# A mixer and a recurrence put into one program, and four small products moved from VectorE to ScalarE

## The reference

```python
x = norm(x + mamba2(x, W_in, conv_w, conv_b, A_log, D_skip, dt_bias, norm_w, W_out))
x = norm(x + bounded_linear(x, weight, scale))     # out = x @ weight * scale, its row norm squashed by tanh and held under 0.99
x = norm(x + rg_lru(x, w_y, w_x, conv, w_ig, w_ag, a_param, w_out))
x = norm(x + gated_ffn(x, gate_w, up_w, down_w))   # integer weights minus 128, silu(g) * u
```

## Time and profile before

| | us |
|---|---|
| median of 3 runs | 1288.69 (1288.57 to 1290.66) |
| the profiled execution | 1291.74 |
| its span, from the first instruction to the last | 1290.0 |
| busy: TensorE, its weight loads, VectorE, ScalarE, GpSimd | 1109.6, 970.0, 779.7, 523.8, 312.8 |
| mean granted clock of TensorE | 0.933 of 2.4 GHz |

### The profile page before, as it was taken

How to read it: one execution, slowest core, us unless ns; L and a number is a source line. 1 busy time by engine, 2 the same in 40 slices (tenths; PEclk the granted TensorE clock), 3 DMA queues, 4 the chain that set the end, 5 groups by cost and what they waited for, 6 DMA issues and landing times. The chain is left out here.

```text
span 1290.0 us, 18165 instructions
## 1 busy us (share of the span) xinstructions
PE 1109.6 (86%) x6912; PEld 970.0 (75%) x6912; DVE 779.7 (60%) x1335; ACT 523.8 (41%) x934; POOL 312.8 (24%) x450
## 2 busy tenths in 40 slices
PE   5689889898989885477899999992899999999998
PEld 5568777877878774367898888982687887878876
DVE  4598888888888888345777766754343323223213
ACT  4564536354545543145545655452231231230320
POOL 1011112020202115144433334410131231230330
PEclk9789999999989996778999999997799999999999
DMA  4403031212213042510000111000900201101001
GB/s 173 161 17 120 10 128 41 88 50 80 88 42 109 4 160 83 211 67 1 33 4 31 33 34 34 14 20 20 347 1 25 73 1 33 65 0 41 25 1 49
DMA packets 41585, 81.15 MB, mean 63 GB/s; under 512 B 7456, under 2 KB 13472, under 8 KB 39456
## 3 DMA queue, kind: packets, MB, share of 16 engines
q1 hardware_dynamic: 41504, 80.06, 17.9%
HBM read 67.19 MB, written 12.85 MB: 62 GB/s over the span
## 5 line engine op out<-in xcount | busy, mean ns | idle before, releaser
L1715 DVE SCALAR_TENSOR_TENSOR d_h<-d_psu,d_us,d_sg 128x512 f32<-128x512 f32 x64 | 48.1, 751 | 168.7 <-PE d_psu L1756 160.0
L1677 ACT ACTIVATE d_sg<-d_psg,d_gs 128x512 f32<-128x512 f32 x64 | 44.1, 690 | 245.3 <-PE d_psg L1756 245.3
L1652 POOL TENSOR_TENSOR d_hl<-d_h,d_hh 128x512 fp32r<-128x512 f32 x64 | 82.8, 1293 | 167.7 <-ACT d_hh L1666 167.7
L552 DVE SCALAR_TENSOR_TENSOR a_xs<-a_xpre,a_cvec,a_xs 128x256 f32<-128x256 f32 x192 | 100.8, 539 | 9.2 <-ACT a_xs L446 4.6
L1768 PE MATMUL d_pso<-d_wd,d_hh 128*128 128x512 f32 x256 | 101.0, 395 | 2.9 <-POOL d_hl L1652 2.9
L1768 PE MATMUL d_pso<-d_wd,d_hl 128*128 128x512 f32 x256 | 100.5, 392 | 0.0
L326 POOL TENSOR_TENSOR a_sg<-a_sg 128x512 f32<-128x512 f32 x16 | 21.2, 1327 | 251.2 <-ACT a_sg L438 251.2
L649 DVE TENSOR_TENSOR_SCAN a_L<-a_L,a_ident 128x512 f32<-128x512 f32 x64 | 81.7, 1338 | 0.5
L789 PE MATMUL a_psr<-a_xth,a_wgh 128*128 128x256 f32 x256 | 74.7, 292 | 7.6 <-DVE a_wgl L543 7.6
L789 PE MATMUL a_psr<-a_xth,a_wxh 128*128 128x256 f32 x256 | 74.9, 293 | 7.0 <-DVE a_wxl L543 7.0
L789 PE MATMUL a_psr<-a_xth,a_wgl 128*128 128x256 f32 x256 | 72.6, 284 | 0.0
(11 more groups left out here) (302 smaller groups left out, 3237.4 us busy)
## 6 DMA issues: line engine op xcount, KB each, us to landing
a_L<-decays SPq DMA_DIRECT2D x16, 1024.0 KB, 4.8
a_xf<-in_x SPq DMA_DIRECT2D x16, 256.0 KB, 2.8
a_xr<-in_x SPq DMA_DIRECT2D x16, 256.0 KB, 2.7
tokens<-a_xr SPq DMA_DIRECT2D x16, 256.0 KB, 2.0
c_xb<-tokens SPq DMA_DIRECT2D x16, 256.0 KB, 2.8
tokens<-c_xb SPq DMA_DIRECT2D x16, 256.0 KB, 2.0
d_xin<-tokens SPq DMA_DIRECT2D x16, 256.0 KB, 4.5
d_wd_codes<-in_down_w SPq DMA_DIRECT2D x4, 1024.0 KB, 15.7
```

The source lines that it names most:

```text
L552: ins = dve.scalar_tensor_tensor(out=dst, in0=src[:, k:k + T], scalar=vec[:, k:k + 1], in1=dst, op0=ALU.mult, op1=ALU.add)
L1652: pool.tensor_tensor(hl[:, m, :], h32[:, m % 2, :], hh[:, m, :].bitcast(F32), ALU.subtract).then_inc(s_hl, 1)
L1677: act.activation(sg[:, m % 2, :], ps_g[:, m % 2, :], ACT.Silu, scale=gs[:, m:m + 1]).then_inc(s_sg, 1)
L1715: dve.scalar_tensor_tensor(out=h32[:, m % 2, :], in0=ps_u[:, m % 2, :], scalar=us[:, m:m + 1], in1=sg[:, m % 2, :], op0=ALU.mult, op1=ALU. ...
```

## The change

It does five things.

1. **One program.** `mamba2` and `bounded_rg_lru` no longer open blocks of their own; each returns a function per engine, and `build` runs them behind each other in one block. No barrier, no reset of semaphores lies between them. They share PSUM (one tensor of 8 banks, cut the same way as far as the steps go), the identity and the constants. The places in SBUF are laid out anew so that the first tiles of the recurrence lie on tiles of the mixer that are free early.
2. **The last step takes in the front of step 0**, from `turn_in` to `turn`, and the softplus: the calls are written between those of the mixer on each engine. All six weights go through the ring of pieces; the last two are split at the end of the front, on ScalarE and then GpSimd.
3. **`tokens` is moved from VectorE to ScalarE**: 8 operations of 128x64 with a scale from `dt` take the place of one of 128x512.
4. **Weights at the start.** The loads of w_bc and of three pieces of w_x go ahead of the small vectors, the halves of w_x ahead of the first `bc`, the halves of w_gate between the first evictions and taps.
5. **Waits.** A helper `Order` lets an engine wait for the instruction that it has just issued. It replaces single semaphores; in `scan` and `cumulate` there is now such a wait behind each scan instead of one behind the last.

The core of the diff (changed indentation left out):

```diff
+class Order:
+    def __call__(self, ins):
+        self.count += 1
+        ins.then_inc(self.sem, 1)
+        self.eng.wait_ge(self.sem, self.count)
...
 # mamba2, SyncE
-            load_piece(0)
+        for i in range(4):
+            load_piece(i)
             for dst, src in ((cvec, conv), (nega, ...), (dtb, ...), (dsk, d_skip), (nrm, norm_w)):
                 sp.dma_start(dst, src).then_inc(s_small, 16)
-            for i in range(1, NG):
+        for i in range(4, NG):
                 load_piece(i)
...
             sp.wait_ge(s_gate, 4 * NS)
-            for i, (raw, src, _, _) in enumerate(following):
-                sp.dma_start(raw, src).then_inc(s_next[i], 16)
+        following_stage["load_x"](0)
+        following_stage["constants"]()
+        load_piece(NW)
+        load_piece(NW + 1)
+        following_stage["load_x"](1)
+        load_piece(NW + 2)
+        load_piece(NW + 3)
+        sp.wait_ge(s_yp, R * C * NS)
+        sp.wait_ge(s_su, G * C * NS)
+        load_piece(NW + 4)
+        load_piece(NW + 5)
             store(NS - 1)
...
 # mamba2, ScalarE
+        def tokens(s, q):
+            act.wait_ge(s_xtr, 4 * s + q + 1)
+            ...
+            for j in range(C):
+                for i in range(HQ):
+                    h = q * HQ + i
+                    ins = act.activation(xdt[:, j, h * HD:(h + 1) * HD], ps_t[:, q % 2, 2 * j + i // 2, i % 2 * HD:(i % 2 + 1) * HD],
+                                         ACT.Copy, scale=dt[:, j, h:h + 1])
+            ins.then_inc(s_xdt, 1)
...
+            else:
+                high_piece(NW)
+                high_piece(NW + 1)
+                following_stage["turn_in"](0)
...
+        square(C * NS - 2)
+        high_y(C * NS - 1)
+        square(C * NS - 1)
+        following_stage["softplus"](0)
+        following_stage["square"](0)
+        high_piece(NW + 2)
+        following_stage["tanh"](0)
+        high_piece(NW + 3)
+        following_stage["softplus"](1)
+        following_stage["turn"](0)
+        following_stage["turn_in"](1)
+        high_piece(NW + 4)
+        high_piece(NW + 5)
...
 # mamba2, VectorE
                 for q in range(Q):
-                    dve.tensor_tensor_scan(own, own, ident4..., 0.0, ALU.mult, ALU.add).then_inc(s_sc, 1)
+                order(dve.tensor_tensor_scan(own, own, ident4..., 0.0, ALU.mult, ALU.add))
...
-            def tokens(s, q):
-                dve.wait_ge(s_xtr, 4 * s + q + 1)
-                dve.tensor_tensor(xdt[:, :, 256 * q:256 * q + 256]..., ps_t[:, q % 2]..., dt[:, :, heads(q)]..., ALU.mult).then_inc(s_xdt, 1)
...
 # mamba2, GpSimd
+        low_piece(NW)
+        low_piece(NW + 1)
+        following_stage["constants"]()
+        tree(C * NS - 2)
+        tree(C * NS - 1)
+        scale(C * NS - 2)
+        scale(C * NS - 1)
+        following_stage["bound"](0)
+        norm(C * NS - 2)
+        following_stage["bounded_norm"](0)
+        norm(C * NS - 1)
+        low_piece(NW + 4)
+        low_piece(NW + 5)
...
 # mamba2, TensorE
-            pe.wait_ge(s_const, 15 + HQ)
+        pe.wait_ge(s_const, 2)
             turn(0)
+        pe.wait_ge(s_const, 15 + HQ)
...
+            else:
+                following_stage["turn_in"](0)
...
+        following_stage["project"](0)
+        out_proj(C * NS - 2, 0)
+        ...
+        out_proj(C * NS - 1, 1)
+        following_stage["turn"](0)
+        following_stage["turn_in"](1)
...
 # bounded_rg_lru, what begins behind the mixer
+        def main():                     # SyncE
+            sp.wait_ge(*last["output"])
+            sp.dma_start(bo, b_out.partition_broadcast(P)).then_inc(s_bias, 16)
+            load_x(2)
```

More of the change, by code:

```diff
@@ L973, in bounded_rg_lru @@
-def bounded_rg_lru(nc, signals, x_in, x_out, scale, vectors, b_out, fill, W, late, space, ahead):
+                        last = pe.matmul(ps_y[:, r, 2 * g + i, :], S[rows(r), b, g, i * P:(i + 1) * P], ex[rows(r), g, cols(j)],
+                                         start=(g, i) == (0, 0), stop=False, skip_group_check=True)
+            last.then_inc(s_in, 1)
+            for r in range(R):
+                pe.wait_ge(s_mx, R * n + r + 1)
+                for g in range(G):
+                    for i in range(HQ):
+                        h = g * HG + r * HQ + i
+                        last = pe.matmul(ps_y[rows(i % 2), r, 2 * g + i // 2, :], xdt[:, j, h * HD:(h + 1) * HD], L[j][:, h, :],
+                                         start=False, stop=True, skip_group_check=True)
+                last.then_inc(s_yp, 1)
@@ new lines, in tensor @@
+        pe.wait_ge(s_const, 2)
+        turn(0)
+        pe.wait_ge(s_const, 15 + HQ)
+        pe.wait_ge(s_wlo, 1)
+        bc(0)
+        turn_z(0)
+        x_proj(0, 0)
+        x_proj(0, 1)
+        for s in range(NS):
+            x_proj(s, 2)
+            if s:
+                out_proj(C * s - 2, 0)
+            turn_a(s)
+            if s:
+                out_proj(C * s - 2, 1)
+            x_proj(s, 3)
+            gram(s)
+            if s:
+                sum_sq(C * s - 2)
+                sum_sq(C * s - 1)
+            x_turn(s, 0)
+            if s:
+                out_proj(C * s - 1, 0)
+                out_proj(C * s - 1, 1)
+            x_turn(s, 1)
+            gate(s, 0)
+            x_turn(s, 2)
+            gate(s, 1)
+            x_turn(s, 3)
+            gate(s, 2)
+            gate(s, 3)
+            if s + 1 < NS:
+                turn(s + 1)
+            state(C * s)
+            scan_out(C * s)
+            if s + 1 < NS:
+                bc(s + 1)
+                turn_z(s + 1)
+                x_proj(s + 1, 0)
+            else:
+                following_stage["turn_in"](0)
+            state(C * s + 1)
+            if s + 1 < NS:
+                x_proj(s + 1, 1)
+            scan_out(C * s + 1)
@@ new lines, in tensor @@
+        following_stage["project"](0)
+        out_proj(C * NS - 2, 0)
+        out_proj(C * NS - 2, 1)
+        sum_sq(C * NS - 2)
+        sum_sq(C * NS - 1)
+        out_proj(C * NS - 1, 0)
+        out_proj(C * NS - 1, 1)
+        following_stage["turn"](0)
+        following_stage["turn_in"](1)
+    last = {"transposes": (s_xdt, 4 * NS), "projections": (s_sg, 4 * NS), "residual": (s_res, C * NS), "mean_sq": (s_rv, C * NS),
+            "gate": (s_gate, 4 * NS), "output": (s_op, C * NS), "stored": s_st, "n_stored": 16 * NS}
@@ L977, in bounded_rg_lru @@
+    split = [(s_nlo, 1), (s_nlo, 2), (s_wlo, NW + 1), (s_wlo, NW + 2), (s_nlo, 3), (s_nlo, 4)]
+    return (sync, gpsimd, scalar, vector, tensor), last, split, (scan_at, scan_end, sb.end)
+def bounded_rg_lru(nc, signals, psum, ident, powers, x_in, x_out, scale, vectors, b_out, W, split, last, spaces, ahead):
     T = 256
@@ L1479, in _ @@
             output(NS - 1)
+        return {"turn_in": turn_in, "project": bounded, "turn": turn, "main": main}
+    return sync, gpsimd, scalar, vector, tensor
 ZERO_POINT = 128.0
```

2156 lines of the change are left out of this document (1036 added, 1120 removed).

## The result

The changed kernel takes 1214.89 us, the median of 4 runs (1211.35 to 1218.3), beside 1288.83 for the kernel before: a ratio of 0.9423, 95% interval 0.9389 to 0.9457, 74 us less. 1225 had been said, in a range of 1208 to 1247. The profiled execution is the fastest of the four, 1211.35 us with a span of 1209.6; that of before had 1291.74 and 1290.0. So the direction and the place are right and three of the four terms close to size, but the steps of the mixer gave half as much again as I had said.

A forecast was written before the change was run, and what follows sets the result against it. Waits between nearly full TensorE and VectorE were taken to decide. Terms 16.9 + 18.9 + 22.9 + 5.3 = 64.0 us off the profiled 1291.74 gave 1227.7, less 3.05 for the median: 1225, range 1208 to 1247 (8 in 10).

The forecast's parts named there:

- A: Start and step 0: earlier weight splits and no wait for `a_ex` save 13.9 + 3.0 = 16.9 us.
- B: Mixer steps 1 to 6: moving `tokens` off VectorE brings `a_ex` earlier, saving 3.15 us a step, 18.9 us.
- C: Tail of step 7 and the recurrence's front: its first projection comes earlier, 22.9 us with step 7's own gain.
- D: Step 0 of the recurrence: taps start 1.5 us later and end 5.4 earlier, saving 5.3 us.
- rival 5: Start: loads, not the order, set it, so only the 3 us of `a_ex` remain; 1239 us, chance 0.06.
- The `a_ex` part of A: Step 0: `a_ex` is ready at 47, before TensorE comes at 52.1, so its 3.04 us wait goes.
- The limit of 0.37: ScalarE's moved products in mixer steps: at 0.37 us of pitch each, the time available for them is just gone.
- Rivals 1 and 4: ScalarE decides the steps: products at 0.37 us lose B, 1244 (chance 0.07); at 0.56, slower than before, 1293 (0.02).
- rival 3: Tail: `update` 14 gets ahead of GpSimd and escapes the exclusion; 8 us more gain, 1217 us, chance 0.13.
- rival 2: Front not hidden: its chain and the mixer's add up, C is 10 us smaller; 1235 us, chance 0.17.

## Why the prediction was right, and where not

The lead of the changed kernel over the kernel before at four marks of the two traces gives each term. The first transpose of z of step 1 is 16.5 us earlier, of step 7 43.9, the recurrence's first projection 69.5, its first gate projection 75.5.

| term | forecast | measured |
|---|---|---|
| A, start and step 0 | 16.9 | 16.5 |
| B, steps 1 to 6 | 18.9 | 27.4 |
| C, rest of step 7 and front | 22.9 | 25.5 |
| D, step 0 of the recurrence | 5.3 | 6.0 |
| behind that | 0 | 4.9 |

The forecast time was 1225 and the median is 1214.89: 10 us less. In the traces B is 8.5 us above its forecast, the largest part of the difference.

**A** was right in sum by two errors that cancel. The first x projection came at 14.48 (13.2 forecast: the loads came in later), the gates at 35.04 (35.5), and `scan_out` of step 0 at 49.87 (52.1). That is 2.2 us better than forecast, then a wait of 4.20 us that I did not name; the way from `scan_out` to the next step was only 2.65 us longer for it (10.62 against 7.97), since before it had begun at a clock of 0.50. The wait comes about because moving the splits of w_gate and w_x forward makes TensorE early, while those of w_out stay where they are on ScalarE, in front of the read of the state. The order by itself is worth 11 us by the ratios and 13.9 at the start of step 1, so rival 5 is out. The `a_ex` part of A was put down to the wrong cause: not the earlier start but the moved products take the 3.04 us away. With the new start and the products on VectorE the wait is still 3.00 us (unchained scans), and with the old start and the products on ScalarE it is gone.

**B** is the term that failed in size. Two things were wrong in its working. First, 3.15 us a step with 0.3 left of the wait; the wait went wholly, and the steady step lost 3.5. The end of `a_ex` came 2.5 us earlier in the step (50.50 + 0.69 before, 47.99 + 0.69 after, from the transpose of z), less than my 3.2. But TensorE comes to it 1.6 us later in the step (49.32 against 47.76 us behind the transpose of z) and needs 1.6 us less from there to the next one (5.13 against 6.77), since the stretch at a lower clock is now ahead of it and no longer behind:

```profile
194.00:198.00 4.00, 3.01 (x19) 2.69 (x18) 3.82 (x10) 3.06 (x8) 0.26 (x1) 0.84 0.52 187
198.00:202.00 4.00, 4.00 (x14) 3.18 (x14) 3.78 (x11) 2.21 (x9) 2.08 (x4) 0.73 0.13 33
```

So `a_ex` is 0.64 us ahead of TensorE, where I had left it 0.3 behind. Second, and worth more: I took all six steps as 58.0. Two of them were 61.67 and 60.87, at 0.94 and 0.92 of the clock, and these 6.5 us above 58 went as well: 27.4 is 6 times 3.5 and 6.4. I had taken one step for all.

The two steps were long for different reasons. Step 1 took as long from `a_ex` to its end as a steady one (6.78 and 6.77 us); 2.4 us of its excess come ahead of `a_a`, with waits of 1.59 and 0.45 us for VectorE, and 1.3 where the clock is 0.80 (101 to 109). The products on ScalarE alone bring it to 56.70, and the changed kernel, with its new start, to 54.59. The step from 312.98 lost 1.6 us ahead of `a_ex`, at a clock of 0.90 (331 to 348), and 1.3 behind it, at 0.61; the products alone remove this. Why this one fell and its neighbours, with waits of 3.74 and 3.49 us, fell less stays open, and with one trace of the kernel before it is not known whether its other runs have such a step. The run with the products back shows the same at a larger size: 0.5 us more of wait goes with 3.3 us more of step.

The price of the chained waits was near (5.00 us for four scans against 4.57, so 0.14 us a wait where 0.11 was said, and 0.86 us ahead of `a_ex` where 0.65 to 0.7 was said), but it costs nothing measurable once TensorE does not wait. The Trainium skill says of eight copies that the semaphore behind each costs nothing extra ("VectorE: DVE Perf Modes", The DRAIN you can't avoid). For these scans, where the engine also waits for each semaphore, the runs show otherwise: 5.00 against 4.57 us for four, and 61.3 against 58.0 us for the step.

**ScalarE** was right throughout: 0.20 of pitch, and nothing on the path. The limit of 0.37 was not reached; at 0.35, with the doubled products, a first wait of 0.47 us appears and the steps stay as long. Rivals 1 and 4 are out.

**C** was right in size while one of its steps was not. `update` 14 did get ahead of GpSimd (rival 3): w_b's high half ended at 447.34, and the update was done at 445.4. But the 8 us that the rival gave it did not come, since the exclusion fell on `update` 15 instead, which the rival had not counted: 5.25 us beside the low half of w_x, and 0.88 with that half on another engine. The Trainium skill's rule that such operations exclude each other for a whole operation ("SBUF — State Buffer", Who interferes with whom) is borne out by that run. The last low half of y ended 28.3 us behind the last gate's eviction (31.5 said) and the recurrence's first projection 27.5 us behind it (28.7 said). Of the 4.4 us won by this 1.7 are lost again: the last gate comes later in step 7 than before (47.6 against 45.9 us behind the transpose of z). The chain of small handovers was placed rightly (VectorE's mean squares 8.6 us behind that low half, both forecast and measured), and rival 2 is out: the overlap by itself is worth 11 us, as the run without it showed.

**D** was right, with a wait of 2.64 us for `c_cvh` where 3 was said.

**The 4.9 us behind** were not forecast. Two steps of the recurrence after, and the same two before:

```profile
597.57:635.83 38.26, 35.86 (x258) 33.38 (x257) 27.73 (x49) 22.07 (x40) 14.34 (x25) 1.00 0.09 28
635.83:674.07 38.24, 35.87 (x259) 33.38 (x257) 27.55 (x49) 22.07 (x40) 14.35 (x23) 1.00 0.10 29
```

```profile
674.48:713.37 38.89, 36.73 (x258) 34.22 (x257) 27.99 (x50) 22.09 (x40) 14.46 (x24) 1.00 0.09 28
713.37:753.36 39.99, 38.22 (x258) 35.70 (x257) 27.18 (x48) 21.88 (x40) 14.27 (x23) 0.96 0.09 27
```

The instructions are the same, and the recurrence's steps vary in other traces too (38.10, 38.43 and 40.17 us one behind the other in the run with the order at the start as before), so it is not put down to the change. The two traces lie 6.4 us further apart than the medians, so these 4.9 us need not be in the result at all: 74 us by the medians against the 64 forecast.

## What to carry to other kernels

Work out a gain from every repetition of a step and not from one: a window for each, with the clock, shows which are longer and why. Where the clock falls behind a wait of TensorE, a microsecond on the engine that it waits for can be worth several (here 0.86 us ahead of `a_ex` made 3.3); where it does not wait, the same microsecond is worth nothing that could be measured. When work is moved forward, look at what stays behind in the same engine's list between it and what the next engine needs; and when low-priority work is moved out of that place, look for whom it is now late.
